# Cross attention and a routed feed-forward layer: another order in the first pair of heads, one transposition moved, and TensorE's program aligned to blocks of 256 instructions

## The reference, cut to what matters

```python
x = x + xattn(layernorm(x), ctx, mask, bias, Wq, Wk, Wv, Wo)
#   q = (hidden_q @ Wq), k = (hidden_kv @ Wk), v = (hidden_kv @ Wv), 32 heads of 128
#   score = einsum('bqhd,bkhd->bhqk', q, k) * scale + position_bias
#   probs = softmax(where(mask, score, -inf));  ctx = probs @ v;  return ctx @ Wo
x = x + ffn(layernorm(x), base_W, base_b, router_W, router_b, A, B, expert_map)
```

## Time and profile before

| | us |
|---|---|
| median of three runs (796.79 to 797.59) | 797.21 |
| the profiled execution: its time | 795.04 |
| the profiled execution: its span | 793.3 |
| PE busy in that span | 778.4 |
| DVE, ACT, POOL busy | 523.3, 399.9, 184.9 |

### The profile page before, as it was taken

The page is one execution under the profiler, slowest core; times in us unless marked ns, Lnnn a source line. Parts: engine busy times, 40 slices in busy tenths (PEclk is TensorE's granted clock), DMA queues, the critical chain, the costliest instruction groups (busy, mean ns, idle before and its releaser), DMA issues.

```text
span 793.3 us, 16707 instructions
## 1 busy us (share of the span) xinstructions
PE 778.4 (98%) x6360; PEld 652.7 (82%) x6360; DVE 523.3 (66%) x951; ACT 399.9 (50%) x1138; POOL 184.9 (23%) x203
## 2 busy tenths in 40 slices
PE   9999999999999999889999999999999999999998
PEld 7888888888888888768888888888888888887886
DVE  6883626267677666477767776677667676657974
ACT  5663525245555555555664466545654466436520
POOL 0225041033433334232211221212211221000200
PEclk9999999999999999999999999999999999999999
DMA  6536773244645547473563356435553455442002
GB/s 226 198 121 220 224 247 135 110 137 159 193 162 157 179 143 225 155 233 118 160 183 112 107 164 183 130 113 159 161 164 117 120 160 175 109 115 85 1 5 103
DMA packets 108077, 118.38 MB, mean 149 GB/s; under 512 B 44239, under 2 KB 77007, under 8 KB 107998
## 3 DMA queue, kind: packets, MB, share of 16 engines
q1 hardware_dynamic: 107998, 117.31, 47.4%
HBM read 81.64 MB, written 35.65 MB: 148 GB/s over the span
## 4 chain that ended last, share of the span: by engine, by line
PE 95%; DVE 2%; issue 1%; ACT 1%; DMA 0%; ACTq 0%
PE pY L1391 42%; PE pP L1391 40%; PE pY L1547 4%; PE pO L1572 2%; PE pT_ L1572 1%; PE pO L1391 1%; PE pT_ L1557 1%; PE pS L1557 1%; PE pS L1572 1%; ACT pr L757 1%; DVE st L977 1%; PE pS L1437 0%; PE pO L1437 0%; DVE y L1126 0%; PE pY L1464 0%
## 5 line engine op out<-in xcount | busy, mean ns | idle before, releaser
L757 ACT ACTIVATE pr<-pr,mx 128x64 f32<-128x64 f32 x256 | 86.2, 343 | 29.7 <-DVE mx L1143 29.7
L1126 DVE TENSOR_TENSOR y<-y,pY 128x512 f32<-128x512 f32 x124 | 84.5, 681 | 23.9 <-PE pY L1391 23.6
L1391 PE MATMUL pY<-wo_hi,oT_hi 128*128 128x512 f32 x248 | 97.0, 391 | 0.5 <-issue 0.5
L1391 PE MATMUL pY<-wo_lo,oT_hi 128*128 128x512 f32 x248 | 96.7, 390 | 0.0
L1391 PE MATMUL pY<-wo_hi,oT_lo 128*128 128x512 f32 x248 | 96.6, 389 | 0.0
L907 DVE TENSOR_TENSOR wk_lo<-wk_raw,wk_hi 128x256 fp32r<-128x256 f32 x96 | 49.3, 514 | 61.6 <-ACT wk_hi L649 60.4
L1391 PE MATMUL pP<-xo_hi,wk_hi 128*128 128x512 f32 x210 | 83.5, 398 | 4.1 <-DVE stage L928 2.1
L649 ACT CAST wk_hi<-twk 128x256 fp32r<-128x256 f32 x128 | 50.8, 409 | 65.1 <-PE pP L1391 54.7
L1391 PE MATMUL pP<-xo_lo,wk_hi 128*128 128x512 f32 x210 | 81.9, 390 | 0.0
L1391 PE MATMUL pP<-xo_hi,wk_lo 128*128 128x512 f32 x210 | 81.9, 390 | 0.0
L582 POOL TENSOR_TENSOR bias<-bias,madd 128x512 f32<-128x512 f32 x32 | 41.1, 1300 | 151.4 <-DMA bias<-in_fside_Bx32xSxS 151.4
(11 more groups left out here) (282 smaller groups left out, 1882.0 us busy)
## 6 DMA issues: line engine op xcount, KB each, us to landing
v_hbm<-stage SPq DMA_DIRECT2D x64, 256.0 KB, 2.3
k_hbm<-stage SPq DMA_DIRECT2D x64, 256.0 KB, 3.6
k<-k_hbm SPq DMA_DIRECT2D x16, 1024.0 KB, 5.3
v<-v_hbm SPq DMA_DIRECT2D x16, 1024.0 KB, 7.0
wk_raw<-in_L_xattn_Wk SPq DMA_DIRECT2D x16, 512.0 KB, 4.5
wo_raw<-in_L_xattn_Wo SPq DMA_DIRECT2D x16, 512.0 KB, 3.6
bias<-in_fside_Bx32xSxS SPq DMA_DIRECT2D x128, 64.0 KB, 3.5
wk_raw<-in_L_xattn_Wq SPq DMA_DIRECT2D x16, 512.0 KB, 4.7
```

The source lines that it names most:

```text
L757: nc.scalar.activation(pr[s][:, b, :], pr[s][:, b, :], ACT.Exp, bias=mx[:, s, b:b + 1], accum_out=sm[:, s, b:b + 1]).then_inc(exp_made, 1)
L1126: nc.vector.tensor_tensor(y[:, t, :], y[:, t, :], src[:, :], ALU.add).then_inc(y_added, 1)
L1391: mm = nc.tensor.matmul(bank_, a, b, start=first and n == 0, stop=last and n == len(terms) - 1, skip_group_check=read_between)
```

## The change

Three edits. In the first pair, block `QB` = 33 takes its own banks (pY0 and pY1, the ones of `scores`), its products are interleaved with those of block 32, the first product of block 34 is done ahead of the pair, and ScalarE's and VectorE's lists are reordered to fit.

```diff
@@ QA = NV + NK
+QB = QA + 1
-ORDER += [(QA, 3), (QA, 4)]
-for n_ in range(QA + 1, NBLK):
+ORDER += [(QA, 3), (QB, 1), (QA, 4), (QB, 2), (QB, 6), (QB, 7), (QB, 5), (QB + 1, 1), (QB, 3), (QB, 4)]
+ORDER += [(QB + 1, p) for p in (2, 6, 7, 5, 3, 4)]
+for n_ in range(QB + 2, NBLK):
     ORDER += [(n_, p) for p in (1, 2, 6, 7, 5, 3, 4)]
@@ x_bank, y_bank
-            return pP[0] if n > QA else (pP[0], pY[0])[n % 2]
+            return pP[0] if n > QB else (pP[0], pY[0])[n % 2]
@@ ScalarE, first pair
-            copy_c12(n)
             exp(0, 0)
-            exp(0, 1)
-            higher(w, 5)
-            exp(1, 0)
-            exp(1, 1)
-            higher(w, 6)
...
             copy_c12(n)
             higher(w, 5)
+            copy_p1(QB)
+            exp(0, 1)
             higher(w, 6)
+            exp(1, 0)
+            higher(w2, 0)
+            copy_u(QB)
+            exp(1, 1)
+            higher(w2, 1)
+            higher(w2, 2)
+            copy_v(QB)
+            higher(w2, 3)
+            higher(w2, 4)
+            wo_high(0)
+            copy_p1(QB + 1)
+            copy_c12(QB)
@@ TensorE, waits
-                    before = n - 1 if n > QA else n - 2
-                    if n == 2:
+                    before = n - 1 if n > QB + 1 else n - 2
+                    if n == QB:
+                        pe.wait_ge(s_read, p)
+                    elif n == 2:
@@ scores
                 elif m == 1:
-                    pe.wait_ge(s_read, s + 1)
+                    pe.wait_ge(c21_made if s else c12_made, QB + 1)
@@ TensorE, first pair and the loop over pairs
             times(n, 3)
+            times(QB, 1)
             times(n, 4)
-            for p in (1, 2, 6, 7, 5, 3, 4):
-                times(n + 1, p)
+            for p in (2, 6, 7, 5):
+                times(QB, p)
+            nc.tensor.addr_align(256, offset=142)
+            times(QB + 1, 1)
+            times(QB, 3)
+            times(QB, 4)
 
             for i in range(NP - 2):
                 turn_p(h)
-                turn_p(h + 1)
                 scores(h + 2)
                 scores(h + 3)
+                turn_p(h + 1)
                 times_v(h)
                 times_v(h + 1)
-                for p in (1, 2, 6, 7):
+                for p in (1, 2) if i else (2,):
+                    times(n, p)
+                if i % 3 == 2:
+                    nc.tensor.addr_align(256, offset=18)
+                for p in (6, 7):
                     times(n, p)
```

More of the change, by code:

```diff
@@ L260, in x_bank @@
         def x_bank(n):
-            return pP[0] if n > QA else (pP[0], pY[0])[n % 2]
+            return pP[0] if n > QB else (pP[0], pY[0])[n % 2]
         def y_bank(n):
-            return pP[1] if n > QA else (pP[1], pY[1])[n % 2]
+            return pP[1] if n > QB else (pP[1], pY[1])[n % 2]
         def first_turn(j):
@@ L791, in _ @@
             n, w, late = QA, next_set(QA), late_set(QA)
+            w2 = next_set(QB)
             copy_p1(n)
@@ L838, in _ @@
                 o_high(h + 1, 0)
-                copy_p1(n)
+                if i:
+                    copy_p1(n)
                 o_high(h + 1, 1)
@@ L1186, in _ @@
             biased(0)
-            make_c22(n)
             largest(0)
@@ L1190, in _ @@
             largest(1)
+            make_c22(n)
             lower_w(w, 4)
@@ L1193, in _ @@
             make_c21(n)
-            n, w2 = QA + 1, next_set(QA + 1)
             lower_w(w, 6)
-            make_c11(n)
-            invert(0)
+            make_c11(QB)
             lower_w(w2, 0)
-            weights(0)
-            weights(1)
             lower_w(w2, 1)
             lower_w(w2, 2)
+            invert(0)
+            weights(0)
+            make_c22(QB)
+            weights(1)
             lower_w(w2, 3)
-            make_c22(n)
             lower_w(w2, 4)
             lower_wo(0)
+            make_c21(QB)
             lower_w(w2, 5)
-            make_c21(n)
             lower_w(w2, 6)
@@ L1664, in _ @@
             turn_p(h)
+            scores(h + 2)
             turn_p(h + 1)
-            scores(h + 2)
             times_v(h)
```

13 lines of the change are left out of this document (3 added, 10 removed).

## The result

The changed kernel takes 790.52 us in the median of 7 runs (788.77 to 793.04), the kernel before 796.79 (793.87 to 797.7, 7 runs beside them). The ratio is 0.9925, with a 95% interval from 0.991 to 0.9941: 6.0 us faster. The profiled execution took 791.96 us with a span of 790.1. The same kernel run again later gave 790.22 us, ratio 0.9928 (0.9908 to 0.9948), and a span of 788.4. Three executions far above all others (1305 and 1580 us in two of the experiments, 972 of the kernel before) count as slow and are in no ratio.

A forecast was written before the change was run, and what follows sets the result against it. TensorE's work and gaps were taken to bound the kernel (PE 95% of the span); -3.5 + 0.4 + 1.4 - 2.6 - 1.0 - 1.1 + 0.2 = -6.2 us, against the 797.21 median 791.0, range 787.8 to 794.2.

The forecast's parts named there:

- First pair, -3.5 and +0.4: First pair: reordered queues start `times_v` near 348.4 with one product done ahead, 3.5 us won; late `make_c11` loses 0.4.
- The 0.4 for the late `make_c11`: Behind the first pair: only product 2 stands between `times_v` and 6 and 7, so 0.4 us lost (0 to 0.8).
- Moved transposition, +1.4: Every pair: second head's transposes moved from before the scores to before `times_v`, 0.10 us in each of 15 pairs lost.
- one step of 0.43 becomes one of 0.53: Transposes in each pair: the step ahead of other transposes becomes one ahead of `times_v`, 0.10 us more.
- The feared wait for the second copy: Second `times_v` in every pair waits for ScalarE's copy; margin 0.12 us; at 0.7 a pair 799.7 us; slower case, chance 0.04.
- Alignment in the regular pairs, -2.6: Regular pairs: paddings move instruction-block edges within `times_v`; of 2.9 us of stalls 0.3 stay, gain 2.6 (1.9 to 2.9).
- The need was 2.6 to 2.7 in four of six: Block fetches before: time needed in us, 3.1 and 3.3 in the other two; about 3.0 available, so it holds mostly.
- First-pair stall, -1.0: First pair's `times_v`: of 1.6 us lost at the block edge 0.6 stays, gain 1.0 (0 to 1.6).
- Last pair but one, -1.1: Last pair but one: edge moves to 86 instructions into `times_v`; of 2.1 us stall 1.0 stays, gain 1.1 (0 to 2.1).
- Paddings, +0.2: 88 empty instructions between TensorE's products cost 0.2 us in all (nothing to 1.5).
- the first pair gives less: Rival, chance 0.15: loads and VectorE hold `times_v` until after 349.5, or the fetch stall there stays whole; 793 us.
- The edges don't matter: Rival, chance 0.10: gaps are not block edges or edges don't move as counted, so alignment gives nothing; 795.7 us.

The follow-up runs named there:

- The last experiment: Changed kernel with transposes moved only each third pair, ScalarE's casts first, and second pair's wo load behind k and bias loads: 786.62 us, ratio 0.9883.
- the transposition alone: Kernel before with only the second head's transposes moved behind both scores, without new first pair or alignment: 795.09 us, ratio 0.9998.
- the three with the casts first: Changed kernel, last-but-one pair's ScalarE casts before exponentials; transposes back, or moved each third pair, or the latter with wo loaded later: 787.84, 787.69, 786.62 us.
- the first pair alone: Kernel before with only the first pair's banks, lists and blocks 32 to 34 changed; no alignment, no moved transposes: 792.07 us, ratio 0.9961.

## Why the prediction was right

The forecast was 791.0 us, and 790.5 came. But of the seven terms only two or three had their size. The two that were too good, the moved transposition and the stall of the first pair, cost 2.4 us more than thought, and about 1 us came from something that the sum didn't have, the clock. That the time was hit to half a microsecond is in part luck.

- **First pair, -3.5 and +0.4.** In the traces 350.55 - 347.72 + 1.36 = 4.2 us, of which 0.44 came about ahead of the pair, where the two programs are the same: 3.75. The second trace gives 3.9 by the same measure (it was 0.42 late ahead of the pair, so 3.5 without it). Alone the part measured 3.1 (1.7 to 4.5). The walk through the queues had the right waits, those for `make_c21` and for v. They were smaller than thought: I took 0.2 for `make_c22`, 0.8 for `make_c21` and 0.2 for v, and measured were none, 0.33 and 0.35 (none, 0.33 and 0.2 in the second trace). The 0.4 for the late `make_c11` did not come: the product ahead was covered.
- **Moved transposition, +1.4.** The mechanism held, the size was 2.8: 0.19 in each of 15 pairs, not 0.10. The step that failed is "one step of 0.43 becomes one of 0.53". The way out of the scores was read rightly (2.016 us to the transposes, 2.015 to `times_v` before). But the step into `times_v` takes 0.585 here, not the 0.53 of the earlier trace rows, which is 0.15 in all, and the products behind are 0.04 longer (the first four take 5.61 us in place of 5.58), which the sum didn't have. Why is open. The feared wait for the second copy did not come.
- **Alignment in the regular pairs, -2.6.** It gave 1.8 in one trace and 2.5 in the other. "The need was 2.6 to 2.7 in four of six": in the changed kernel 3.0 to 3.4 us passed. The need is no constant. From the packet's start to the restart it is 2.2 to 3.0 us in all stalls of all traces. What varies more is when the packet starts: 0.0 to 1.0 us behind the opening of the block in the regular pairs' stalls, up to 3.4 in the first pair and in the last but one, where loads fill the DMA engines.
- **First-pair stall, -1.0.** Nothing was won: 1.85 us stayed, against "I let 0.6 of the 1.6 us lost there stand". The prediction had named the cause, the loads that fill the engines, and left it out of the size. The last experiment bears it out.
- **Last pair but one, -1.1.** The size is about right (2.14 - 0.64 = 1.5 in both traces, as long as the clock stays; in the first trace its fall took the 1.5 back), the reason is not. "I leave 1.0" stood for a rest of the fetch stall; the fetch stall went altogether, and what stands there is the wait for VectorE's `o_lo`, which had been hidden behind it. Where a stall goes, I had not asked what is late next in this place.
- **Paddings, +0.2.** Nothing in the changed kernel.

Terms as measured in the second trace of the changed kernel: first pair and what lies ahead of it -3.5, transposition in 14 pairs +2.6, edges in the regular pairs -2.5, first-pair stall -0.1, last pair but one with its own transposition -1.4: -4.9 us, and the spans differ by 793.3 - 788.4 = 4.9. So the sum of -6.2 was 1.3 too good against the profiled execution of before. The medians differ by 6.3 and, the second time, 6.0: that execution of before was 1.7 us under its own median. Most of the rest is the clock. The granted clock, as a mean over the execution, is on record for 70 executions of the kernel before and 13 of the changed kernel:

| | executions | median, us |
|---|---|---|
| before, mean clock 0.999 or more | 21 | 794.8 |
| before, below that (to 0.991) | 49 | 796.6 |
| before, all | 70 | 796.1 |
| changed, mean clock 0.999 or more | 9 | 789.8 |
| changed, all | 13 | 790.3 |

At the full clock the kernels differ by 5.0 us, as the two spans do. The seven executions of before at 0.991 have a median of 799.1. A stretch at half the clock like the one at 715 us is worth 0.002 of the mean (an estimate from its 3 us in 790), so these had several. So about 1 us of the 6 goes with the clock, which falls less often in the changed kernel: in 4 of 13 executions where it was 49 of 70. (They ran on several chips, and the executions with a low clock may have longer stalls too, which no trace of before shows.) The prediction had no such term. The first pair's wait of 2.06 us, which the change removes, is one place where it fell (the trace of the transposition alone). Of the kernels without the new first pair 29 of 93 executions kept the full clock, of those with it 55 of 76 (the one with 223 empty instructions not counted), and of the three with the casts first all 18. Of the rivals, "the first pair gives less" happened in its second half (the stall stays whole) without its first. "The edges don't matter" is refuted: with every layout that was tried the stalls stood at its own edges, and with all edges 102 instructions into `times_v` none was left behind the first pair. The Trainium skill (Runtime: NRT & Kernel Launch, Instruction fetch mechanics) calls the crossing mostly hidden. Of 51 crossings in the kernel before seven were not, 6.9 us in all; for the others the sentence agrees with the trace.

The sum of the parts taken alone is -3.1 - 0.2 - 1.3 = -4.6 us, the whole -6.0 and -5.7. That the parts help each other (the moved transposition gives room to the edges that the alignment leaves) is possible and not shown; the difference is within the intervals.

## What to carry to other kernels

Where the chain shows pieces called issue at no fixed place, count instructions: if they end at one remainder of 256, they are fetches, and in these traces they cost time only where 256 instructions are used up in some 3 us or less, or where loads fill the DMA engines just when a block is opened. In the second case a load that can wait (here wo) was the better lever than the layout of the program: with it the whole stall was gone (0.8 us at the edge), with no empty instruction and nothing moved on TensorE.

A stall that is removed uncovers the next wait of the same place. Before you price it, look at when each semaphore of the instructions behind it is given: here the order of five lines on ScalarE was worth 1.2 us in the trace, half of what the alignment gave.

Compare kernels execution by execution with the mean clock beside the time. A short wait can cost more than its length when the clock falls behind it, and a change that removes waits then gives more than a profile at full clock shows: here about 1 of 6 us.

## What the runs showed of the hardware

- A wait that is already fulfilled costs TensorE nothing, even as an instruction of its own in a stretch of 64x64 matmuls: six of them out of each pair left the period at 25.55 us.
- An empty instruction costs 0.06 to 0.07 us once the product ahead no longer hides it: 223 left a gap of 14.2 us, 39 one of 1.1 (0.9 more than the usual step), 27 none in the changed kernel. In the traces one starts 0.071 us behind the other. 22 cost 0.17 to 0.29 in one other kernel, and why is open.
- The granted clock fell to about half (the level of 1.2 GHz) for some 3 us behind short idle times of TensorE: 0.64 us at 713.5 in the first trace of the changed kernel, 2.06 us at 334 in that of the transposition alone, 2.17 us at 709.4 in that of the first pair alone. It did not fall behind the same 2.06 us or the 1.88 us of the earlier trace rows in the trace of before, nor behind the same 0.64 us in the second trace of the changed kernel. What decides it stays open. One fall cost 1.5 us.
- The same program in the same place stalls by 0.43 us in one execution and 0.19 in another. One trace gives the place of a fetch stall, not its size.
